# Where the attention mask is put into PSUM: by a ScalarE copy, or by an identity matmul on TensorE

## The reference, cut to what matters

```python
s1 = jnp.einsum('bhqd,bhkd->bhqk', q1, k1) * scale
s2 = jnp.einsum('bhqd,bhkd->bhqk', q2, k2) * scale
allowed = (j <= i) & (j >= i - WINDOW + 1)          # WINDOW = 64
s1 = jnp.where(allowed[None, None], s1, NEG)         # NEG = -1e30
s2 = jnp.where(allowed[None, None], s2, NEG)
a1 = jax.nn.softmax(s1, axis=-1)
a2 = jax.nn.softmax(s2, axis=-1)
diff = jax.nn.relu(a1 - lam[None, :, None, None] * a2)
diff = diff / (jnp.sum(diff, axis=-1, keepdims=True) + 1e-06)
out = jnp.einsum('bhqk,bhkd->bhqd', diff, v)
```

## Time and profile before

| | |
|---|---|
| time, median of 3 runs | 1395.27 us (1394.65 to 1396.21) |
| the profiled execution | 1395.27 us, span from first to last instruction 1393.4 us |
| mean granted TensorE clock | 0.978 of full speed |
| busy, whole span | PE 1309.9, PEld 1026.1, DVE 847.0, ACT 722.3, POOL 470.7 us |
| stage A | about the first 510 us of the span; 64 units |
| chain that ended last, by engine | PE 71%, issue 12%, DVE 6%, ACT 4%, POOL 4% |

### The profile page before, as it was taken

How to read it: one execution, slowest core, us unless ns; L and a number is a source line. 1 busy time by engine, 2 the same in 40 slices (tenths; PEclk the granted TensorE clock), 3 DMA queues, 4 the chain that set the end, 5 groups by cost and what they waited for, 6 DMA issues and landing times.

```text
span 1393.4 us, 27992 instructions
## 1 busy us (share of the span) xinstructions
PE 1309.9 (94%) x9948; PEld 1026.1 (74%) x9948; DVE 847.0 (61%) x1985; ACT 722.3 (52%) x2767; POOL 470.7 (34%) x466
## 2 busy tenths in 40 slices
PE   5899999999999888999999999959999999999998
PEld 3677887887887765666676666548888888888887
DVE  7788788787887576646646656755443343333433
ACT  2788887887887554444444444453333242333322
POOL 3222122212211134534534534550044253432532
PEclk9899999999999899999999999988999999999999
DMA  6011002000102101001002001010134234253130
GB/s 213 16 32 39 17 17 54 17 16 16 32 16 88 34 1 73 1 2 73 2 1 72 1 1 59 1 40 18 33 70 132 63 93 90 38 132 75 43 100 30
DMA packets 29684, 64.57 MB, mean 46 GB/s; under 512 B 6784, under 2 KB 12032, under 8 KB 28288
## 3 DMA queue, kind: packets, MB, share of 16 engines
q1 hardware_dynamic: 29568, 63.05, 16.3%
HBM read 52.42 MB, written 2.23 MB: 39 GB/s over the span
## 4 chain that ended last, share of the span: by engine, by line
PE 71%; issue 12%; DVE 6%; ACT 4%; POOL 4%; DMA 2%; SPq 1%; POOLq 0%; DVEq 0%; ACTq 0%
PE ps L515 30%; PE ps L879 9%; PE ps L698 4%; PE ps L802 4%; PE ps L631 4%; PE ps L663 3%; PE ps L792 3%; PE ps L776 3%; PE ps L784 2%; PE ps L674 2%; POOL ea L1622 2%; PE ps L654 2%; DMA cw<-comb_d 2%; ACT ea L1392 1%; PE ps L570 1%
## 5 line engine op out<-in xcount | busy, mean ns | idle before, releaser
L1751 POOL TENSOR_TENSOR sg<-sg,cw 128x512 f32<-128x512 f32 x88 | 113.6, 1291 | 278.6 <-ACT sg L1558 270.6
L1333 DVE TENSOR_TENSOR hh<-ps,sg 128x512 f32<-128x512 f32 x100 | 69.2, 692 | 182.1 <-POOL sg L1751 165.6
L1359 ACT ACTIVATE hhh<-hh 128x512 fp32r<-128x512 f32 x100 | 63.2, 632 | 209.0 <-DVE hh L1333 198.2
L1359 ACT ACTIVATE pt<-ps 128x512 f32<-128x512 f32 x128 | 76.8, 600 | 179.3 <-PE ps L784 112.9
L1392 ACT ACTIVATE ea<-ps,negmax 128x64 f32<-128x64 f32 (+1 forms) x512 | 164.6, 341 | 6.0 <-DVE negmax L1085 6.0
L515 PE MATMUL ps<-xnh,wch 128*128 128x512 f32 x400 | 159.6, 399 | 0.5 <-DVE x_sb L1046 0.5
L515 PE MATMUL ps<-xnh,wcl 128*128 128x512 f32 x400 | 159.3, 398 | 0.0
L515 PE MATMUL ps<-xnl,wch 128*128 128x512 f32 x400 | 158.5, 396 | 0.0
L1132 DVE TENSOR_TENSOR qcs<-ps,tabb 128x512 f32<-128x512 f32 x192 | 123.5, 686 | 54.6 <-PE ps L515 54.2
L1622 POOL TENSOR_TENSOR ea<-ea,rden 128x128 f32<-128x128 f32 (+1 forms) x128 | 62.2, 507 | 230.8 <-DVE rden L1041 230.8
L1629 POOL TENSOR_TENSOR eb<-eb,rsum 128x512 f32<-128x512 f32 x64 | 66.5, 1039 | 172.7 <-DVE rsum L1172 172.7
(11 more groups left out here) (149 smaller groups left out, 3436.6 us busy)
## 6 DMA issues: line engine op xcount, KB each, us to landing
raw_w<-in_rawb_dram SPq DMA_DIRECT2D x4, 2432.0 KB, 9.4
kva<-ktmp SPq DMA_DIRECT2D x64, 128.0 KB, 2.3
cw<-comb_d SPq DMA_DIRECT2D x32, 256.0 KB, 4.8
raw_w<-in_rawc_dram SPq DMA_DIRECT2D x4, 1920.0 KB, 8.1
cw<-comb_d SPq DMA_DIRECT2D x16, 224.0 KB, 4.2
raw_a<-in_wqk_dram SPq DMA_DIRECT2D x4, 768.0 KB, 4.5
cw<-comb_d SPq DMA_DIRECT2D x16, 192.0 KB, 5.9
cw<-comb_d SPq DMA_DIRECT2D x16, 160.0 KB, 5.5
```

The costliest lines, as they stand in the source:

```text
L1333: dve.tensor_tensor(hh[:, par, :], bank(C_U[par]), sg[:, par, :], ALU.mult).then_inc(c_h, 1)
L1359: return act.activation(dst, src, ACT.Copy)
L1751: pool.tensor_tensor(sg[:, par, :], sg[:, par, :], cw[:, c % 2, t, :], ALU.mult).then_inc(c_hs, 1)
```

## The change: the mask by TensorE in every unit

The ScalarE copy and its semaphore go. TensorE issues the two identity matmuls in every unit, ahead of the scores of the map that they belong to, and waits before the first of them for the exponentials of two units before (`a_ex` at n-1, which is the last read of the same banks) in place of the copy.

```diff
-        a_mk = sem("a_mask_in_place")
...
-                    wait(pe, a_mk, n - 1)
+                    wait(pe, a_ex, n - 1)
                     tok = slice(S * j, S * (j + 1))
                     for m in range(2):
                         sc = A_S[u % 2][:, m, 0:SW]
-                        if first and u < 2:
-                            pe.matmul(sc, idb[:, :], maskb[:, :], start=True, stop=False, skip_group_check=True)
+                        pe.matmul(sc, idb[:, :], maskb[:, :], start=True, stop=False, skip_group_check=True)
                         for at, to, keys in ((QH, late(sc), S), (0, early(sc), QH)):
...
-                if not drain and not (final and u >= UN - 2):
-                    act.wait_ge(a_ex, n + 1)
-                    copy(A_S[u % 2][:, :, 0:SW], maskb[:, :].unsqueeze(1).broadcast_to([128, 2, SW])).then_inc(a_mk, 1)
```

## The result

| | before | changed |
|---|---|---|
| median | 1395.74 us (1394.65 to 1396.25, 4 runs) | 1418.66 us (1417.41 to 1419.37, 4 runs) |
| profiled execution, span | 1393.4 us | 1416.2 us |
| mean granted clock | 0.978 | 0.981 |
| busy PE / ACT | 1309.9 / 722.3 us | 1343.2 / 678.0 us |

The ratio is 1.0166, with a 95% interval of 1.015 to 1.0182: the kernel is slower by 22.9 us. The forecast was 25.0 us.

What follows compares the result with a forecast made beforehand. TensorE was taken to pace stage A, with ScalarE having time left. New pairs 30.9 us, less 4.6 and 0.5 absorbed by waits and 0.75 for unit 2, gave +25.0: 1420.3 us from 1395.3, range 1409 to 1432.

Steps and rivals of the forecast that it cites:

- Price of a pair: Stage A, TensorE: two mask matmuls cost 0.67 - 0.09 - 0.07 = 0.51 us a unit at full clock.
- the change over to L515: Unit 0's second score half: 0.07 us of its 0.82 belong to the following L515, so were taken off the pair.
- entering the scores: Step from L515 into the score matmuls: 0.09 us extra, in future paid by the mask matmul, so taken off the pair.
- The load ahead: Mask matmul behind an L515: its weight load, 0.10 us or so, taken as hidden; decides 0.1 us a unit.
- The gap rule: Skill page's matmul gap: 162.5 ns for 384 columns, 20 us for 124 matmuls; rows 4 disagreed with 250 and 270 ns.
- rival (a): Stage A mask matmuls: only streaming counts, a pair costs 0.34 us; +16.5, 1411.7 us; chance 0.13.
- What the waits absorb: TensorE's long GpSimd waits shrink: 3 x 1.53 = 4.6 us between 60 and 420 us, 0.5 more in the last group.
- Unit 2 of the first group: Mask copy there delays ScalarE's layer-norm copies, for which TensorE waits; its removal takes 0.75 us off.
- Rival (c): Granted clock: falls may come or go elsewhere, -5 to +8 us on the forecast; chance 0.07 for its part below 1415.
- The last two units: End of stage A: both run at a low granted clock, so their pairs cost 2 x 0.92 = 1.8 us.
- Its own signs of being wrong: Stage A grows under 17 or over 33 us, non-GpSimd waits change over 3 us in sum, or growth lies in low clock.
- two hidden pairs: Units 12 and 13 of the last group: TensorE's waits for VectorE's low weights, 5.1 us in three, hide two pairs.

Runs made afterwards that it cites:

- narrow mask: Changed kernel with the mask matmul cut from 384 to 128 columns from the third unit on; 1409.45 us against 1396.71 for the kernel before, ratio 1.0084.
- the version with adjacent masks: Changed kernel with both mask matmuls of a unit issued ahead of all 16 score matmuls; 1406.16 us against 1396.71 for the kernel before, ratio 1.0069.
- The version with pairs in the waits: Kernel before with adjacent TensorE masks replacing copies in units 9, 10, 12 of every group and unit 2 of the first; 1392.29 us against 1395.64, ratio 0.997.

## Why the prediction was right

**TensorE paces stage A and ScalarE does not.** It held. The removal from ScalarE alone is worth 3.3 us, the addition on TensorE alone costs 25.6.

**Price of a pair.** Forecast 0.51 us at full clock, measured 0.60. The step that failed is the one that took 0.07 us off, as "the change over to L515". The second half of the scores takes 218.29 - 217.47 = 0.82 us with the transposes behind it as well, and the earlier trace rows already had the same for the first half, with a mask behind it (29.80 - 28.98 = 0.82). So the excess belongs to any half block that stands alone, whatever follows: two of them take 1.65 us and the undivided block 1.49. Cutting the block in two costs 0.16 us, all of it the mask's. The other deduction, 0.09 for entering the scores, held: L514 to mask takes 0.24, where 0.23 was predicted, and not 0.32. The pair thus adds up from rows: 0.52 for the two mask steps, 0.16 for the cut, less 0.08, is 0.60. On 57 units the 0.09 us by which the price was too low are worth 5.1 us, 4.0 of them by this step.

**The load ahead.** The price was as if it were hidden, but the trace does not show it ahead: it is recorded at 216.12, at the start of its own matmul, and still the step to that matmul is 0.24 us, 0.01 over the step from L515 to L515. So the price read off was right, while the way to it, a load that starts ahead as that of an L515 does, is not what happened.

**The gap rule.** The Trainium skill, "TensorE: Matmul & The Clock Gate", "Back-to-back issue gap" (N/2.4 + 2.5 ns), gives 162 ns for 384 columns. The narrow mask agrees with its slope, 0.10 to 0.11 us for 256 columns, and the adjacent pair takes 0.43 us, of which 0.17 are from mask to mask and 0.26 from mask to scores. What the formula leaves out is here 0.10 us for each step from a mask into the scores, and 0.16 for a block that is cut in two. So rival (a), "only streaming counts", is refuted for this change, at 0.60 us a pair; the version with adjacent masks has that rival's price, 0.35 us for 0.34, though its +9.5 us lie well below the rival's +16.5.

**What the waits absorb.** Forecast: 2.15 and 1.20 shrink by 1.02 and 0.51. Measured: by 1.19 and 0.59, two pairs and one pair of 0.60. The mechanism held, and three groups gave 5.3 us in place of 4.6. The single wait in group 3 gave 0.58, for 0.5 forecast; a later one there grew instead, from 0.68 to 1.43, while the waits on VectorE's low weights fell from 5.1 to 3.2. Unit 2 of the first group gave its 0.75: from its scores to the transposes it took 48.08 - 42.45 = 5.63 us and takes 46.99 - 42.12 = 4.87.

**The clock.** Rival (c) came true in its good half. In stage A the lower clock was granted for 30.7 us before (seven stretches) and 20.5 us after (four stretches, up to TensorE's last output projection at 542.8). At half speed that is worth up to 5.1 us. It hides the error in the price: +5.1 us by the one, up to -5.1 by the other. So the mechanism was right, but that the number came out within 2.1 us is in part luck: two errors cancel. The budget from the profiles is 62 x 0.60 = 37.2, less 9.1 for waits from 60 us on (27.4 us in sum before, 18.3 after), less 1.4 for the wait of the earlier trace rows, less 5.1 for the clock: 21.6 us, against 22.8 in the spans.

The last two units were forecast at the lower clock, and one of them was. The second-last has 0.44 us from mask to scores; the last one's masks, at 515.59 and 516.67, have 0.26 and 0.27, the full clock.

```profile
504.91 0.50 PE L625 MATMUL ps<-maskb,idb 128*128 128x384 bf16 x1
505.35 1.55 PE L629 MATMUL ps<-kva,qab 128*64 128x128 f32 x16
506.83 0.50 PE L625 MATMUL ps<-maskb,idb 128*128 128x384 bf16 x1
```

**ScalarE's busy time** fell by 44.3 us and not by 53. The copies overlap their neighbours in the record: the one at 45.20 is 0.81 us long, and the next begins after 0.75 (45.95, `xnf`). With that, 62 x 0.75 = 46.5, and 2.2 us stay open. Taking an engine's busy time apart by durations overstates it by such overlaps.

**Its own signs of being wrong.** One was met: other waits than GpSimd's should not change by over 3 us in sum, and they fell from 14.5 to 10.6 (60 to 500 us before, 60 to 520 after; 0.6 of it is a wait that now lies just ahead of 60). Half of that is the wait for VectorE's low weights (5.1 to 3.2), which the prediction had counted as two hidden pairs. The prediction also speaks of two long waits in each group; the last group has one, of 2.16 us, as its own sum has it.

## What to carry to other kernels

An operation moved from an engine with time left to the one that paces the stage costs its full price there, and its removal from the other gives next to nothing. Where it has to be, price its neighbours too: in the middle of a block of scores the pair cost 0.60 us, directly ahead of the block 0.35, and between two blocks of projections 0.08. And look first for the waits of the pacing engine that hang on nothing of its own: work put there cost 0.0 to 0.1 us for three pairs, where three pairs elsewhere cost about 1.0.

## What the runs showed of the hardware

The granted clock fell behind TensorE's waits for GpSimd in a pattern that the profiles tell, not prove. Four places of stage A have the long wait (one in each group). In the nine profiles of this case it was 2.14 to 2.17 us long at 11 of these 36 places (four before, four with no mask at all, three with masks in units 4, 6 and 8), and the clock fell at 6 of them. At the other 25 it was 0.96 to 2.01 us long, and the clock fell at one (the narrow mask, a wait of 1.78). One fall costs 1.6 us, as the unit steps show. The length of one wait does not decide it alone: in the last units of the last group the clock fell in all nine profiles, and there the waits just ahead, for VectorE and GpSimd, were often below 2.0 us, such as 1.43 us in the changed kernel. The version with pairs in the waits was built on this and gained what was expected, 3.4 us, of which 0.75 have another cause; the split of the rest between the clock and the small gains of ScalarE's relief was not measured apart. A wait on the pacing engine can thus cost more than its length, and filling it can give back more than nothing.
